# A graph network on one core: the first buffer of the summation layers apart and loaded early, their first two pieces mixed, and the rescaling of a node on ScalarE

## The reference

```python
# layer 0: attention with edge features, 8 heads
alpha = leaky(sum(h_src * a_src) + sum(h_dst * a_dst) + sum(relu(edge_attr @ W) * h_dst))
ex = exp(alpha - segment_max(alpha, dst)[dst])
out = segment_sum(h_src * ex / segment_sum(ex, dst)[dst], dst)
# layers 1 to 3: mean of the neighbours' rows (relu between them)
agg = segment_sum(x[src], dst) / degree
h = agg @ Wl + b + x @ Wr
# layer 4: the sum over neighbours and the node itself, both sides scaled by 1/sqrt(degree)
out = relu(segment_sum(h[src] * norm, dst) + b)
```

## Time and profile before

| | |
|---|---|
| median of 3 runs | 3315.35 us (3314.17 to 3328.64) |
| the profiled execution's own time | 3314.46 us |
| its span | 3312.6 us |
| TensorE matmul busy | 2700.5 us (82%) |
| VectorE busy | 1819.1 us (55%) |
| ScalarE busy | 1223.2 us (37%) |
| GpSimd busy | 1470.2 us (44%) |
| mean granted clock of TensorE | 0.884 of full speed |

### The profile page before, as it was taken

How to read it: one execution, slowest core, us unless ns; L and a number is a source line. 1 busy time by engine, 2 the same in 40 slices (tenths; PEclk the granted TensorE clock), 3 DMA queues, 4 the chain that set the end, 5 groups by cost and what they waited for, 6 DMA issues and landing times.

```text
span 3312.6 us, 50756 instructions
## 1 busy us (share of the span) xinstructions
PE 2700.5 (82%) x12657; PEld 1721.4 (52%) x12658; DVE 1819.1 (55%) x4880; ACT 1223.2 (37%) x3147; POOL 1470.2 (44%) x1469
## 2 busy tenths in 40 slices
PE   6997998989989999999997997466677747766765
PEld 4774555555655545545555555344455535544543
DVE  6996999999962010000005005466666547666665
ACT  2774555555521001001001002644444454444445
POOL 5402766666613004004005001777777347777760
PEclk8998999999979999999998999777777868788785
DMA  7456877777712322322321332455545235555541
GB/s 230 130 125 171 225 214 207 206 219 209 211 21 82 100 63 77 98 70 67 101 77 62 104 98 63 131 140 136 136 136 143 77 109 136 140 141 139 138 114 40
DMA packets 310915, 421.17 MB, mean 127 GB/s; under 512 B 56707, under 2 KB 245047, under 8 KB 310367
## 3 DMA queue, kind: packets, MB, share of 16 engines
q1 hardware_dynamic: 235679, 231.06, 24.2%
q0 software_dynamic: 60544, 173.03, 19.6%
q10 hardware_dynamic: 14400, 13.93, 1.4%
HBM read 378.03 MB, written 39.84 MB: 126 GB/s over the span
## 4 chain that ended last, share of the span: by engine, by line
PE 43%; POOL 17%; issue 15%; DVE 14%; DMA 4%; ACT 4%; DVEq 2%; SPq 1%; ACTq 1%; POOLq 0%
PE ps L762 24%; POOL rows L2155 17%; PE ps L1002 3%; PE ps L633 3%; DMA rows<-table,src_idx 2%; DVE norm L1344 2%; PE ps L982 2%; PE ps L721 2%; PE ps L612 2%; ACT norm L1173 1%; PE ps L922 1%; DVE al L1350 1%; PE ps L819 1%; DVE segmax L1386 1%; PE ps L932 1%
## 5 line engine op out<-in xcount | busy, mean ns | idle before, releaser
L2155 POOL DMA_INDIRECT rows<-table,src_idx x1248 | 1251.7, 1003 | 511.6 <-issue 367.1
L762 PE MATMUL ps<-rows,rT 128*128 128x448 f16 x2800 | 765.4, 355 | 20.3 <-DMA rows<-adjacency 12.8
L762 PE MATMUL ps<-rows,spread 128*128 128x448 f16 x1400 | 497.1, 355 | 0.0
L762 PEld LDWEIGHTS ps<-rows,rT 128*128 128x128 bf16 x2800 | 275.4, 98 | 281.2 <-issue 29.2
L1556 DVE TENSOR_TENSOR rows<-ps,norm 128x896 f32<-128x896 f32 x21 | 22.9, 1092 | 636.7 <-PE ps L762 636.7
L2109 POOL CAST rT<-rows 128x1024 bf16<-128x1024 f32 (+1 forms) x28 | 30.1, 1074 | 727.6 <-ACT rows L1288 508.9
L819 PE MATMUL ps<-rows,spread 128*128 128x260 f32 x832 | 278.8, 503 | 67.6 <-DVE rows L1667 67.2
L819 PE MATMUL ps<-rows,w_roots 128*128 128x260 f32 x832 | 270.0, 490 | 37.7 <-DVE rows L1667 37.6
L819 PEld LDWEIGHTS ps<-rows,spread 128*128 128x128 f32 x832 | 207.2, 257 | 122.8 <-DVE rows L1667 71.5
L1667 DVE TENSOR_TENSOR rows<-rows,ps 128x1024 f32<-128x1024 f32 x208 | 249.0, 1197 | 30.2 <-issue 25.6
L612 PE MATMUL ps<-rT,spread 128*128 128x264 f32 x832 | 247.1, 422 | 4.1 <-DMA rT<-table 2.1
(11 more groups left out here) (270 smaller groups left out, 4302.5 us busy)
## 6 DMA issues: line engine op xcount, KB each, us to landing
rows<-adjacency SPq DMA_DIRECT2D x140, 560.0 KB, 4.0
rT<-table SPq DMA_DIRECT2D x316, 136.0 KB
spread<-in_tiles SPq DMA_DIRECT2D x104, 256.0 KB, 4.4
rows<-table,src_idx POOLq DMA_INDIRECT x1248
rT<-table ACTq DMA_DIRECT2D x100, 136.0 KB
w_table<-in_tiles SPq DMA_DIRECT2D x52, 256.0 KB
adjacency<-rT SPq DMA_DIRECT2D x4, 2800.0 KB, 13.7
adjacency<-acc SPq DMA_DIRECT2D x3, 2800.0 KB, 13.6
```

The costliest lines, as they stand in the source:

```text
L762: ins = mm(chunk_ps[c % 2][:, f, :], xp[k][:, t, f * P:(f + 1) * P], ring[q][:, i, :], start=t == 0 and k == 0, stop=t == ROWS - 1 and k = ...
L2155: pool.indirect_dma_start(src_rows(l, par)[:, k, :], None, tables[l][:, :], bass.IndirectOffsetOnAxis(ap=src_idx[:, g * T + k:g * T + k + ...
```

## The change

Three things are changed.

1. Buffer 0 of `ring` moves to words 6656 to 7776 of `rows`, between the node stage's tables and the `weighed` buffer; buffers 1 to 4 move down to words 0 to 4480, below the tables. Only one `weighed` buffer is left. Buffer 0 is loaded as soon as the first row of the node stage before is ready, the other four when the last row is.
2. TensorE takes the groups of the first two pieces in the order (0,0) (0,1) (0,2) (0,3) (1,0) (1,1) (1,2) (0,4) (1,3) (1,4); the further pieces follow as before. The counts for which VectorE and SP wait follow this order (USED_AT).
3. In layer 0 rescale_node is done by ScalarE, between encoded(m, 3) and node_sums_out: three ACTIVATEs with a scale out of `resc_f` in place of VectorE's two products. VectorE loses the register load, the two waits and both products.

```diff
-        ring = [rows[:, q * PIECE:(q + 1) * PIECE].bitcast(F16)... for q in range(NQ)]
+        ring_at = [8704 - FC * CC - 32 - PIECE] + [q * PIECE for q in range(NQ - 1)]
+        ring = [rows[:, ring_at[q]:ring_at[q] + PIECE].bitcast(F16)... for q in range(NQ)]
...
-        weighed = [rows[:, 8704 - (b + 1) * FC * CC:8704 - b * FC * CC].rearrange("p (f n) -> p f n", f=FC) for b in range(2)]
+        weighed = rows[:, 8704 - FC * CC:8704].rearrange("p (f n) -> p f n", f=FC)
...
+        SUM_ORDER = [(0, q) for q in range(NQ - 1)] + [(1, q) for q in range(NQ - 2)] + [(0, NQ - 1), (1, NQ - 2), (1, NQ - 1)]
+        SUM_ORDER += [(c, q) for c in range(2, PIECES) for q in range(NQ)]
+        USED_AT = {of: i + 1 for i, of in enumerate(SUM_ORDER)}
...
-            for c in range(PIECES):
-                if c > 1:
+            for c, q in SUM_ORDER:
+                if c > 1 and q == 0:
                     pe.wait_ge(window_added, PIECES * (l - 1) + c - 1)
-                for q in range(NQ):
...
+            def rescale_node(g, par):
+                node = act.value_load(base[0:1, bass.ds(g, 1)], min_val=0, max_val=N)
+                if isinstance(g, int) and g == 0:
+                    act.wait_ge(acc_cleared, 1)
+                act.wait_ge(resc_copied, g + 1)
+                act.wait_ge(added, g + 1)
+                for f in range(FC):
+                    col = acc[:, f, bass.ds(node, 1)]
+                    nc.scalar.activation(col, col, ACT.Copy, scale=resc_f[par][:, f:f + 1])
+                dcol = den[0:H, bass.ds(node, 1)]
+                nc.scalar.activation(dcol, dcol, ACT.Copy, scale=resc_f[par][0:H, FC:FC + 1]).then_inc(rescaled, 1)
...
                     encoded(m, 3)
+                rescale_node(g, j % 2)
                 node_sums_out(g, j)
...
-                node = V.value_load(base[0:1, bass.ds(g, 1)], min_val=0, max_val=N)
-                dve.wait_ge(resc_copied, g + 1)
-                dve.wait_ge(added, g + 1)
-                V.tensor_tensor(col, col, resc_f[par][:, 0:FC].unsqueeze(2), ALU.mult)
-                V.tensor_tensor(dcol, dcol, resc_f[par][0:H, FC:FC + 1], ALU.mult).then_inc(rescaled, 1)
...
-                dve.wait_ge(piece_used, NQ * (before + c + 1))
+                dve.wait_ge(piece_used, NQ * before + USED_AT[c, NQ - 1])
...
                         if c > 0:
-                            sp.wait_ge(piece_used, NQ * PIECES * (l - 1) + at - NQ + 1)
-                        elif q < 3:
+                            sp.wait_ge(piece_used, NQ * PIECES * (l - 1) + USED_AT[c - 1, q])
+                        elif q == 0:
+                            sp.wait_ge(row_ready, ROWS * l + 1)
+                        else:
                             sp.wait_ge(row_ready, ROWS * (l + 1))
-                        else:
-                            sp.wait_ge(parts_ready, NCH * l)
```

More of the change, by code:

```diff
@@ L221, in gnn_program @@
         xp.append(spread[:, :].bitcast(BF16).rearrange("p (t d) -> p t d", t=ROWS))
-        ring = [rows[:, q * PIECE:(q + 1) * PIECE].bitcast(F16).rearrange("p (h c) -> p h c", h=HQ) for q in range(NQ)]
+        ring_at = [8704 - FC * CC - 32 - PIECE] + [q * PIECE for q in range(NQ - 1)]
+        ring = [rows[:, ring_at[q]:ring_at[q] + PIECE].bitcast(F16).rearrange("p (h c) -> p h c", h=HQ) for q in range(NQ)]
         stage_words = [x[:, 0:ROWS * PITCH // 2].rearrange("p (h c) -> p h c", h=ROWS) for x in (low, early)]
@@ L235, in gnn_program @@
         more_adj = rows[:, more_at_end + 2056:more_at_end + 2056 + KEYS // 2].bitcast(F16)
-        weighed = [rows[:, 8704 - (b + 1) * FC * CC:8704 - b * FC * CC].rearrange("p (f n) -> p f n", f=FC) for b in range(2)]
-        more_weighed = weighed[0][:, :, 0:SPAN]
+        weighed = rows[:, 8704 - FC * CC:8704].rearrange("p (f n) -> p f n", f=FC)
+        more_weighed = weighed[:, :, 0:SPAN]
         al = sb("al", [P, 64])
@@ L746, in sum_pe @@
             pe.wait_ge(row_out, ROWS * (l + 1))
-            for c in range(PIECES):
-                if c > 1:
+            for c, q in SUM_ORDER:
+                if c > 1 and q == 0:
                     pe.wait_ge(window_added, PIECES * (l - 1) + c - 1)
-                for q in range(NQ):
[L752 to L755, removed]
-                    else:
[L757 to L764, removed]
+                if c == 0:
+                    pe.wait_ge(parts_ready, NCH * (l - 1) + 1 + -(-(HQ * (q + 1) - 1) // 4))
+                if l not in MEAN_LAYERS and q in loop_rows(c):
+                    pe.wait_ge(loops_added, loops_upto(c, q))
+                else:
+                    pe.wait_ge(piece_landed[q], 16 * (PIECES * (l - 1) + c + 1))
+                for i in range(HQ):
+                    t = HQ * q + i
+                    for f in range(FC):
+                        for k in range(PARTS):
+                            ins = mm(chunk_ps[c % 2][:, f, :], xp[k][:, t, f * P:(f + 1) * P], ring[q][:, i, :],
+                                     start=t == 0 and k == 0, stop=t == ROWS - 1 and k == PARTS - 1)
+                ins.then_inc(piece_used, 1)
             def window(w):
@@ L1397, in messages @@
                 V.tensor_tensor(z, z, x[:, :, 0:H].unsqueeze(3).broadcast_to([P, 4, H, D // H]), ALU.mult).then_inc(msg_ready, 1)
-            def rescale_node(g, par):
-                node = V.value_load(base[0:1, bass.ds(g, 1)], min_val=0, max_val=N)
-                if isinstance(g, int) and g == 0:
-                    dve.wait_ge(acc_cleared, 1)
-                dve.wait_ge(resc_copied, g + 1)
-                dve.wait_ge(added, g + 1)
-                col = acc[:, :, bass.ds(node, 1)]
-                V.tensor_tensor(col, col, resc_f[par][:, 0:FC].unsqueeze(2), ALU.mult)
-                dcol = den[0:H, bass.ds(node, 1)]
-                V.tensor_tensor(dcol, dcol, resc_f[par][0:H, FC:FC + 1], ALU.mult).then_inc(rescaled, 1)
             def add_window(node, par):
@@ L1474, in step @@
                     reductions(m, 2)
-                rescale_node(g, j % 2)
-                if m is not None:
                     products(m, 3)
@@ L1555, in sum_dve @@
                 if mean:
-                    V.tensor_tensor(weighed[c % 2], summed, of_nodes, ALU.mult).then_inc(window_weighed, 1)
+                    V.tensor_tensor(weighed, summed, of_nodes, ALU.mult).then_inc(window_weighed, 1)
                     dve.wait_ge(window_weighed, PIECES * MEAN_LAYERS.index(l) + c + 1)
-                    V.tensor_tensor(acc[:, :, of], acc[:, :, of], weighed[c % 2], ALU.add).then_inc(window_added, 1)
+                    V.tensor_tensor(acc[:, :, of], acc[:, :, of], weighed, ALU.add).then_inc(window_added, 1)
                 else:
```

## The result

| | before | after |
|---|---|---|
| median | 3314.76 us (3309.57 to 3328.64, 4 runs) | 3277.39 us (3273.36 to 3284.06, 4 runs) |
| profiled execution, its span | 3314.46, 3312.6 us | 3273.36, 3271.5 us |
| TensorE, VectorE, ScalarE busy | 2700.5, 1819.1, 1223.2 us | 2694.1, 1804.1, 1241.9 us |
| mean granted clock | 0.884 | 0.882 |

The ratio is 0.9886, with a 95% interval of 0.9858 to 0.9915: faster by 37 us where 41 were forecast.

What follows compares the result with a forecast made beforehand. VectorE was taken to bound the edge loop, TensorE close behind, and a transfer to delay each summation layer. Gains of 18 + 14 + 8.7 = 41 us from 3315.4 gave 3274 us, range 3262 to 3296.

Steps and rivals of the forecast that it cites:

- What bounds the kernel: VectorE sets the edge loop's pace, busy 589 of 628 us; adjacency transfers of about 4 us precede each summation layer.
- Part 1, the size in a group: Layer-0 edge loop: taking the rescaling off VectorE removes 0.42 us from each group, or 0.29 by a narrower reading.
- L623's wait almost goes: Sign in the edge loop: TensorE's wait for VectorE at L623 falls from 0.45 us to about 0.03.
- Part 1, ScalarE: Edge loop: the three added ACTIVATEs take 0.60 us on ScalarE, exactly filling the room of 0.6, without margin.
- Part 1, the sum: Edge loop: 0.36 us kept in each of 50 groups gives 18 us; ends 22 us gained or 68 us lost.
- Part 2: Starts of layers 1 to 4: loading the first group's buffer early saves 3.5 us each, 14 us in all.
- Part 3: Summation blocks of layers 1 to 3: TensorE's clock no longer falls at the start, 8.7 us; bounds 0 to 11.3.
- Part 4: Summation layers: mixed order and single `weighed` buffer cost 0; 3.3 us if reloads take the longest time seen.
- (a): Rival, edge loop: ScalarE becomes the bound and eats the rescaling's gain, time 3292 us; chance 0.18.
- (b): Rival, edge loop: ScalarE's insertion exceeds 1.44 us and groups grow, up to 3360 us; chance 0.07.
- (c): Rival, summation layers: clock falls despite 0.7 us idle, or buffer 4's late reload stalls; 3277 to 3283 us; chance 0.10.
- (d): Rival, summation layers: the early load doesn't shorten the start, as something else was late; 3297 us; chance 0.05.

Runs made afterwards that it cites:

- experiments on the halves: Two kernels: kernel before with only the rescaling moved to ScalarE, 3302.55 us (0.9948); changed kernel with the rescaling back on VectorE, 3301.98 us (0.9935).
- late load: Changed kernel with buffer 0 loaded only when the last row is ready, like the other four: 3302.07 us, 0.9932 of the kernel before.
- no rescaling: Changed kernel without ScalarE's three ACTIVATEs and their register load, so nobody rescales: 3287.35 us, one run.
- fillers: Changed kernel with four useless matmuls per layer-0 group in TensorE's pause: 3269.87 us, 0.9843 of before; with two there, 3272.54 us, 0.9850.
- kernel with both edits: Changed kernel with four useless matmuls per layer-0 group and GpSimd's last layer-4 split held until the first self loops are added: 3266.87 us, 0.9825.
- straight order: Changed kernel with the summation pieces in straight instead of mixed order, early load kept: 3285.37 us, 0.9880 of the kernel before.

## Why the prediction was right, and where it was off

- **What bounds the kernel.** Right: VectorE in the edge loop, a transfer before each summation layer. The experiments on the halves and the late load show both.
- **Part 1, the size in a group.** Right: 0.42 us was worked out from the earlier trace rows, 0.40 came (0.25 in the groups near both ends, which took 11.87 before). The sign "L623's wait almost goes" did not come: 10.7 us in 30 groups were left of 17.3 in 39.
- **Part 1, ScalarE.** Right that it fits, and it did with room: 0.44 us of insertion where I took 0.60, and one wait at L647 for L1112 in the whole loop, 0.5 us, as before. I let ScalarE eat 0.06 of each group; it ate none (no rescaling: 11.61 too).
- **Part 1, the sum.** This term was mis-sized: "0.36 us kept in each of 50 groups ... is 18 us" measured 12 us in after. Without the falls the groups got 17 us shorter together, and the six others another 2. But the falls of TensorE's clock took 0.89 us in each of 14 groups where they had taken 0.54 in each of 7: 12.5 - 3.8 = 8.7 us lost. The group of 14.18 us lost 2.6 more, and the four groups with a jump were 4.3 us shorter together, which is mostly luck, since their lengths scatter in every kernel. The earlier trace rows had the clock at 0.95, which I gave no price. I had also reckoned TensorE's slack of 0.45 us as spare time; it was in use, as cover for the falls. The 12 us are of one execution: the loops of the other kernels with part 1 and no fillers are 9 to 16 us shorter than before's, and part 1's ratio (17 us, 12 to 23) can't tell 12 from 18. That the falls take something back is shown by the fillers, the exact size is not.
- **Part 2.** 3.5 us in layers 1 to 3, as forecast; in layer 4 5.4, since the self loops took 1.45 and not 3.29. That they might was in the text ("up to 2 us more"), but the cause wasn't: GpSimd's split beside them. The text also misread: minimum, median and maximum don't say that 27 of 28 took 0.2 us, and in the trace a second one took 0.97.
- **Part 3.** 8.7 us forecast; the blocks gave 2.68 + 1.65 + 2.91 + 2.09 = 9.3. I gave layer 4 nothing, expecting 4 us of idle time; it was 2.1 us, and the clock was at its upper level. That part is luck as much as reckoning: the clock had just fallen and risen ahead of the gap, and in the kernel with both edits, where it hadn't, 2.35 us of idle time were followed by a fall.
- **Part 4.** Right, 0. The late loads were issued together at 1061 us in layer 1, and the first of them landed after 4.2 us, under the 5.67 that there are; each of the four blocks is 198.8 us, so none waited. The straight order is as fast.
- **The rivals.** (a) is refuted by the kernel without the rescaling, (b) by 0.44 us of insertion against 1.44, (c) and (d) by the blocks of 198.8 us and the starts.

The errors, 6 us too much in part 1 and 2.5 too little in parts 2 and 3, cancel in part: 12 + 16 + 9.3 = 37 us.

The Trainium skill's rule (ScalarE: Activation LUTs, Rules for kernel authors), multiplications on VectorE, would have kept 17 us in the kernel. The prices on the same page (What ACT_TABLE_LOAD costs), 186 ns for an ACTIVATE, 93 ns more for a scale of its own per partition and 93 ns of overlap, give an estimate of 0.28 us for one and of 0.19 us from its start to the next one's. The rows agree: L1106 took 0.28, and L1104 twice 0.47.

What stays open: what sets in which groups the clock falls, in this kernel as a rule every second to fourth, why part 1 makes it fall more often, and why 0.3 us of matmuls in each group nearly ends it.

## What to carry to other kernels

A few microseconds in which TensorE waits for a transfer cost more than half as much again in the clock behind them: of the 25 us that the early load gave in the trace, 9 were clock. Look at the granted clock of a loop before pricing a gain in it: at 0.95 in a loop that TensorE nearly fills, its slack is already spent on falls, and what another engine gains is partly given back. There a few matmuls of no use in TensorE's pause may pay (here 14 us of 3284), while in its busy stretch they pay less (two of them 0.9873 of before's time, against 0.9850 in the pause), as the slack that they use makes each fall that is left dearer.

## What the runs showed of the hardware

- VectorE's fp16 additions of two tensors are held up by GpSimd's subtraction of two tensors and by its cast: 0.60 us for four alone, and beside them 1.45 to 4.43. The instruction that is held up ends just behind GpSimd's (1780.75 and 1780.70 at a subtraction, 1771.14 and 1771.06 at a cast). Not every one is: in after two of about 0.22 us ran before the long one.
- More work made TensorE faster: 4 matmuls of 240 columns in each group brought the mean clock of the loop from 0.93 to 0.98.
- A fall of the clock of the same depth (0.86 or 0.87 over a group) cost 0.5, 0.9 or 1.6 us, by how much TensorE waited for VectorE without it.
- At each of the four jumps back in the hardware loop, VectorE and ScalarE pause for 2.4 to 3.9 us; those groups take 15.2 to 17.6 us in every kernel. No experiment touched them. The Trainium skill (Runtime: NRT & Kernel Launch, Instruction fetch mechanics) says that a taken branch to instructions not held on the engine has to wait for their transfer. That fits in kind; no run here tested it.
